# Column maximum of the router logits: read by VectorE from PSUM in two halves, behind ScalarE's half copies

## The reference, cut to what matters

```
x      = _layernorm(x, norm_g, norm_b)
se     = _layernorm(slot_embeds, slot_g, slot_b) * scale
logits = einsum('bnd,esd->bnes', x, se)          # 2 x 1024 tokens, 1024 slots
dispatch = softmax(logits, axis=1)               # over the 1024 tokens of a batch
combine  = softmax(logits over all 1024 slots)   # over a token's slots
slots = einsum('bnd,bnes->besd', x, dispatch)
... gate/up/down of 16 experts ..., out = combine @ eout
```

## Time and profile before

| | us |
|---|---|
| median of 3 runs | 600.85 (600.81 to 602.04) |
| profiled execution, its own time | 601.5 |
| its span, first to last instruction | 599.8 |
| PE, DVE, ACT, POOL busy in the span | 551.3, 483.7, 394.5, 320.3 |
| logits stage, from the first to the last copy L764 | 308.5 to 362.8 |
| dispatch stage, from the first to the last L1377 | 368.5 to 427.0 |

### The profile page before, as it was taken

One profiled execution on the slowest core, in us unless ns is written; L12 is line 12 of the kernel. 1 busy time (PEld: TensorE's weight loads), 2 busy tenths in 40 slices (PEclk: granted clock), 3 DMA queues, 4 the chain that ended last, 5 costly groups with the idle time before them and its releaser, 6 DMA issues.

```text
span 599.8 us, 11864 instructions
## 1 busy us (share of the span) xinstructions
PE 551.3 (92%) x3880; PEld 507.0 (85%) x3880; DVE 483.7 (81%) x1338; ACT 394.5 (66%) x1054; POOL 320.3 (53%) x327
## 2 busy tenths in 40 slices
PE   5889999999999999999889996999779999969998
PEld 3778999999999999999777765888658788869998
DVE  5888878787889889896859998999798999964553
ACT  3877959696968869695724435566476667555552
POOL 6463753544445644544559867565088999810000
PEclk9999999999999999999999997999889999989999
DMA  7602000000200000000013331050087888604552
GB/s 198 211 2 71 2 2 2 1 2 1 87 3 2 2 1 2 1 2 2 2 72 140 148 133 71 8 208 1 1 267 264 274 281 276 218 35 141 177 176 70
DMA packets 35372, 53.36 MB, mean 89 GB/s; under 512 B 6157, under 2 KB 21457, under 8 KB 35313
## 3 DMA queue, kind: packets, MB, share of 16 engines
q1 hardware_dynamic: 35313, 52.61, 26.3%
HBM read 42.12 MB, written 10.49 MB: 88 GB/s over the span
## 4 chain that ended last, share of the span: by engine, by line
PE 55%; DVE 21%; POOL 9%; ACT 7%; issue 7%; DMA 1%; SPq 0%; POOLq 0%; DVEq 0%; ACTq 0%
PE ps L1447 8%; PE ps L1316 8%; DVE w_gu_low L866 7%; PE ps L1267 6%; PE ps L1300 5%; PE ps L1377 5%; PE ps L1248 5%; PE ps L1279 3%; PE ps L1348 3%; PE ps L1302 2%; PE ps L1436 2%; POOL prob L595 2%; DVE wkq_low L1093 2%; DVE eo_high L1129 2%; ACT expo L726 2%
## 5 line engine op out<-in xcount | busy, mean ns | idle before, releaser
L595 POOL TENSOR_TENSOR prob<-expo,prec 128x512 f32<-128x512 f32 x64 | 66.7, 1043 | 97.3 <-DVE prec L982 96.1
L726 ACT ACTIVATE expo<-expo,nmin 128x154 f32<-128x154 f32 x256 | 106.2, 423 | 4.0 <-DVE nmin L971 3.6
L971 DVE CUSTOM_DVE_ANT_0 expo<-ps,maskb 128x154 f32<-128x154 f32 x256 | 69.1, 312 | 11.8 <-PE ps L1267 11.3
L656 POOL TENSOR_TENSOR wkq_low<-w_raw,wkq_high 128x1024 fp32r<-128x1024 f32 x16 | 51.3, 3207 | 24.5 <-ACT wkq_high L684 24.5
L1267 PE MATMUL ps<-kbd,qT_high 128*128 128x308 f32 x256 | 61.0, 322 | 0.2 <-ACT qT_high L665 0.2
L991 DVE TENSOR_TENSOR pT_low<-ps,pT_high 128x512 fp32r<-128x512 f32 (+1 forms) x96 | 57.3, 597 | 4.2 <-ACT pT_high L740 3.8
L740 ACT CAST pT_high<-ps 128x512 fp32r<-128x512 f32 (+1 forms) x96 | 49.1, 515 | 15.5 <-PE ps L1279 11.8
L665 ACT ACTIVATE oT_high<-ps,bv_c 128x256 fp32r<-128x256 f32 x64 | 29.9, 468 | 36.9 <-PE ps L1302 36.9
L726 ACT ACTIVATION_READ_ACCUMULATOR expo<-expo,nmin 128x1 f32 x256 | 50.3, 196 | 0.0
L866 DVE TENSOR_TENSOR w_gu_low<-w_raw,w_gu_high 128x1024 fp32r<-128x1024 f32 x18 | 46.9, 2615 | 1.2 <-ACT w_gu_high L684 1.2
L1267 PEld LDWEIGHTS ps<-kbd,qT_high 128*128 128x128 f32 x256 | 39.9, 190 | 0.8 <-issue 0.4
(11 more groups left out here) (217 smaller groups left out, 1823.2 us busy)
## 6 DMA issues: line engine op xcount, KB each, us to landing
logits_dram<-lsb SPq DMA_DIRECT2D x16, 512.0 KB, 2.6
w_raw<-in_L_ffn_Wg_dram SPq DMA_DIRECT2D x16, 512.0 KB, 4.4
w_raw<-in_L_ffn_Wu_dram SPq DMA_DIRECT2D x16, 512.0 KB, 4.6
w_raw<-in_L_ffn_Wd_dram SPq DMA_DIRECT2D x16, 512.0 KB, 4.3
lraw<-logits_dram SPq DMA_DIRECT2D x16, 512.0 KB, 3.7
out_dram<-outb SPq DMA_DIRECT2D x16, 128.0 KB, 1.7
x<-in_x_dram SPq DMA_DIRECT2D x1, 1792.0 KB, 13.6
wk_raw<-in_L_xattn_Wk_dram SPq DMA_DIRECT2D x2, 512.0 KB, 5.0
```

The costliest lines, as they stand in the source:

```text
L595: pool.tensor_tensor(prob[:, n % 2, :, heads, :], expo[:, n % 2, pp, :, :, 0:P], prec[:, n % 2, pp].unsqueeze(3).to_broadcast([P, 2, 2, P] ...
L656: pool.tensor_tensor(low, w_raw[:, i % RAW].rearrange("p (k n) -> p k n", k=KD if w == 0 else FT), high, ALU.subtract).then_inc(gate_low i ...
L726: ins = act.activation(row, row, ACT.Exp, scale=-1.0, bias=nmin[:, n % 2, pp, j, h:h + 1], accum_out=psums[:, n % 2, pp, j, h:h + 1])
L971: ins = dve.tensor_tensor_reduce(out=expo[:, n % 2, pp, j, h, :], in0=ps[:, s % NS, h * SK:(h + 1) * SK], in1=maskb[:, (2 * (n // QUADS) + ...
```

## The change

ACT copies each tile in two instructions of 512 columns, one for each bank, and raises `l_ready` after each. DVE waits for each half by itself and folds it into `colmax`, but reads the logits from the PSUM bank and no longer from `lsb`; for the first tile of a batch it copies the bank. `colmax_ready` is raised after the second half. PE's wait for the banks of tile i - 2 now asks for `colmax_ready` instead of `l_ready`, and so does the first expert's. The store waits for both halves. The row maximum still reads `lsb`.

```diff
-            sp.wait_ge(l_ready, i + 1)
+            sp.wait_ge(l_ready, 2 * (i + 1))
...
                 act.wait_ge(l_full, i + 1)
-                act.copy(lsb[:, i].rearrange("p (c n) -> p c n", c=2), ps[:, 2 * (i % 2):2 * (i % 2) + 2, :])\
-                    .then_inc(l_ready, 1)
+                for c in range(2):
+                    act.copy(lsb[:, i, c * 512:(c + 1) * 512], ps[:, 2 * (i % 2) + c, :]).then_inc(l_ready, 1)
...
-                dve.wait_ge(l_ready, i + 1)
-
                 b = i // TB
                 if i % TB:
                     dve.wait_ge(colmax_ready, i)
-                first = lsb[:, i] if i % TB == 0 else colmax[:, b]
-                dve.tensor_tensor(colmax[:, b], first, lsb[:, i], ALU.max).then_inc(colmax_ready, 1)
+                for c in range(2):
+                    dve.wait_ge(l_ready, 2 * i + c + 1)
+                    most, src = colmax[:, b, c * 512:(c + 1) * 512], ps[:, 2 * (i % 2) + c, :]
+                    if i % TB == 0:
+                        ins = dve.tensor_copy(most, src)
+                    else:
+                        ins = dve.tensor_tensor(most, src, most, ALU.max)
+                ins.then_inc(colmax_ready, 1)
...
-                    pe.wait_ge(l_ready, i - 1)
+                    pe.wait_ge(colmax_ready, i - 1)
...
-                    pe.wait_ge(l_ready, TILES)
+                    pe.wait_ge(colmax_ready, TILES)
```

## The result

The changed kernel took 595.01 us (median of 4 runs, 592.82 to 596.76), the kernel before 601.44 beside it (4 runs, 600.81 to 602.08). The ratio is 0.990, 95% interval 0.988 to 0.992: 6 us faster. The forecast was 596.2 with a range from 594.0 to 599.5, on a time before of 600.85. The profiled execution of the changed kernel took 595.16 with a span of 593.4, against 601.5 and 599.8.

A forecast was written before the change was run, and what follows sets the result against it. PE, DVE and POOL were taken as full at once in the logits stage, with DVE and POOL excluding each other over SBUF. Gains 0.7 + 0.3 + 1.4 + 2.2 = 4.6 us, from 600.85 to 596.2; range 594.0 to 599.5.

The forecast's parts named there:

- The root: DVE instructions with two SBUF operands and POOL instructions exclude each other; prediction wrong if POOL's lengths stay.
- Part 1: Engine costs per logits tile: two PSUM halves cost DVE 0.05 us more; its round is 3.08, the same as PE's.
- Part 2: Start of the logits stage: POOL's chain to PE's transposes no longer held up by the first maximum; gain 0.7 us.
- Part 3: Logits tiles 2 to 8: PE keeps its own 3.08 us a tile, six tiles 18.5 instead of 18.75; gain 0.3.
- Part 4: Logits tiles 9 to 14, where DVE is late: shorter diagonal and maxima; gain 1.4 us.
- Part 5: Into the dispatch stage: earlier x_low and three L641 in 7.2 us instead of 9.0; gain 2.2 us.
- Part 6: PE's new wait for the maximum of tile i - 2: at least 1.1 us spare, cost 0.
- The rival "DVE": Logits stage: non-overlapping halves make DVE's round 3.25 against PE's 3.08; 598.2 us; chance 0.20, shared with a stopped gain.
- The slower rival: Logits stage: a POOL instruction slips between two halves, 0.6 us a tile; 606.9 to 609.1, say 608; chance 0.05.
- The clock: First dispatch block: shorter PE idle time keeps its clock up, some 1.0 us comes back, 595.2; chance 0.10.

The follow-up runs named there:

- psum_whole: Kernel before, whole copies and whole 1024-column maxima kept, but the maxima read the PSUM banks: 594.53 us, ratio 0.990.
- sbuf_halves: Changed kernel, but the half maxima read lsb in SBUF and PE gets the banks back from ACT: 606.4 us, ratio 1.009 to the kernel before.
- dve_plus: Changed kernel plus one unused 256-column reduction on DVE per tile: 596.88 us, ratio 0.993 to the kernel before.
- no_shift: Kernel before with POOL's shift addition (L624) left out: 598.26 us, ratio 0.995.
- warm: Changed kernel plus 12 unused identity matmuls on PE ahead of its wait for the last maximum: 593.69 us, ratio 0.987 to the kernel before.
- exp_only: Kernel before with only the dispatch stage's exponentials put in PSUM: 593.22 us, ratio 0.987.
- exp_in_psum: Changed kernel plus dispatch exponentials written to the logits banks, both halves made from there: 586.91 us, ratio 0.977 to the kernel before.
- exp_psum_warm: Changed kernel plus dispatch exponentials in PSUM and 12 filling matmuls on PE: 587.99 us, ratio 0.977 to the kernel before.
- again: Changed kernel once more, unaltered: 595.18 us, ratio 0.990 to the kernel before.
- whole_and_exp: Whole copies, whole maxima from PSUM and dispatch exponentials in PSUM: 589.81 us, ratio 0.982 to the kernel before.

## Why the prediction was right, and where it was off

**The root was right.** DVE with two SBUF operands and POOL exclude each other; reading PSUM ends that. POOL's additions are 0.74, three L641 take 7.05 us (forecast 7.2), and `psum_whole` and `sbuf_halves` show that it is the operand and not the halves. The Trainium skill says in "SBUF — State Buffer", section "Who interferes with whom", that a DVE instruction with two SBUF inputs contends with a GpSimd instruction that reads SBUF. The runs agree: half a maximum has a mean of 1190 ns with two SBUF operands and of 685 with one in PSUM.

**Part 1, right in its price, and lucky in its balance.** The pair costs 1.29 us, as in the earlier trace rows, and DVE holds PE's pace, though with nothing to spare, as `dve_plus` shows. But DVE's round was reckoned at 3.08, the same as PE's, and PE's own is 3.00. DVE keeps up with that only because its round is shorter too: from `x2T_low` to the row maximum it takes 0.65 (320.98 to 321.63) and not 0.75, since the centring between them (L1046) takes 0.41 instead of 0.50. That POOL is the reason is likely, not shown: its instruction then under way ended 0.34 us after the centring's start before (322.34) and ends 0.14 after it now (321.45). Before, then after:

```profile
322.00 0.50 DVE L1046 TENSOR_SCALAR x2f<-x,mv,rstd 128x256 f32<-128x256 f32 x1
```

```profile
321.31 0.41 DVE L1046 TENSOR_SCALAR x2f<-x,mv,rstd 128x256 f32<-128x256 f32 x1
```

The prediction had neither of the two; that they are of one size is luck. The rule that speaks against it (the Trainium skill, "VectorE: DVE Perf Modes", section "The TRN2 errata": a dearer fixed cost from PSUM) is not seen here: 1221 ns with one operand in PSUM, 1.21 to 1.23 us with both in SBUF, for 1024 columns.

**Part 2, right:** 0.81 for 0.7. L611 is 0.20 us, as reckoned.

**Part 3 is the step that failed.** It says "PE keeps its own 3.08"; its own pace is 3.00, as after and as in `no_shift`. Rows 2 show transposes 3.08 apart with no wait in brackets. The wait stands in the rows of the weight loads (PEld), which I did not count: before, the transposes' weight load starts after 0.28 to 0.38 us of idle time, 0.1 us behind the end of POOL's addition, tile after tile; after, it follows without idle time. Before, then after:

```profile
323.77 1.66 POOL L624 TENSOR_TENSOR x2f<-x2f,shift 128x256 f32<-128x256 f32 x1
...
325.54 0.20 PEld L1332 LDWEIGHTS ps<-ident,x2f 128*128 128x128 f32 x2 [0.29 <-issue]
```

```profile
327.65 0.37 PEld L1336 LDWEIGHTS ps<-ident,x2f 128*128 128x128 f32 x2
```

The releaser in the brackets is no help: for some tiles it is "issue", for others `x2T_low`, never POOL. So I took a pace set by POOL for PE's. Six tiles at 3.00 give 0.72 instead of 0.3.

**Part 4: right in kind, two terms too small.** The first rows are of before, the second of after.

```profile
336.22 1.22 DVE L1065 TENSOR_TENSOR colmax<-lsb 128x1024 f32<-128x1024 f32 x1
...
349.80 1.65 POOL L623 TENSOR_TENSOR x2f<-x2f,gain 128x256 f32<-128x256 f32 x1 [3.19 <-DVE x2f L1046]
...
352.39 0.41 PE L1332 MATMUL ps<-ident,x2f 128*128 128x128 f32 x2 [0.17 <-POOL x2f L624]
```

```profile
334.76 1.28 DVE L1066 COPY colmax<-ps 128x512 f32<-128x512 f32 x2
336.67 0.69 DVE L1085 TENSOR_TENSOR diag<-ident,nb 128x512 f32<-128x512 f32 x1
...
345.16 0.42 DVE L851 TENSOR_TENSOR x2T_low<-ps,x2T_high 128x256 fp32r<-128x256 f32 x1
...
345.63 0.73 PE L1352 MATMUL ps<-wkq_high,x2T_high 128*128 128x512 f32 x2 [0.30 <-DVE x2T_low L851]
```

From the maximum of tile 8 to the `x2T_low` that tile 12 waits for, DVE's list took 11.63 us (336.22 to 347.85) and takes 10.40: 1.23, where the diagonal at 0.69 and the shorter maxima had been reckoned at 1.27. But tile 8's maximum also starts sooner after the transposes, 3.88 us (330.88 to 334.76) against 4.40: 0.52, taken as 0.1. DVE's maxima lagged further behind PE before: tile 7's started 1.20 us after its transposes (333.02 after 331.82) and starts 0.89 after them now (331.77 after 330.88). And from tile 12's matmuls to the copy of tile 13 it is 6.94 against 7.30 us: 0.36 that I had not seen. It is the exclusion once more: POOL's multiplication at 349.80 took 1.65 behind a maximum issued at 349.63, and PE waited for POOL's chain at 352.39, which it does not now. Together 2.11 for 1.4.

**Part 5, right:** 2.33 for 2.2. The low half still meets the third L641, and ends 1.1 us after it.

**Part 6, right:** the wait for `colmax` costs nothing that the profile shows.

**The sum** is 1.4 us short: 0.4 from the pace taken for PE's own, 0.4 from DVE's lateness ahead of tile 8, 0.36 from PE's wait for POOL after tile 12, and 0.2 in parts 2 and 5. The pace and the wait for POOL come from the exclusion, which reached further than I had followed it; what made DVE later is not taken apart by any run. The median of the runs, 595.0, lies 1.2 under the forecast; the kernel before measured 601.44 beside it, not 600.85, so the gain is 6.4 where 4.6 was forecast, and 0.4 of that lies outside the stage. The rival "DVE" fell, but by a few hundredths of a microsecond a tile. The slower rival fell for PSUM operands, and stands for SBUF ones: `sbuf_halves` took 606.4, and the rival's lower bound is by its own terms 606.7 (600.85 + 6.3 - 0.43), not 606.9. The clock fell as before, and cost about 0.25.

## What to carry to other kernels

Where DVE and POOL are both busy, look for pairs of rows of which one is long exactly until the other ends; if DVE's instruction can read one of its two operands from PSUM, where it often lies anyway, both run at their own length. Do not count on splitting the instruction as a cure: here two halves in SBUF were worse than one whole (606.4 against 601.2). And before an interval between two matmuls is taken for PE's own pace, look at its weight loads too, and at what ended just before them on the other engines: a wait of a tenth can stand there without its true releaser, and recur each round.

## What the runs showed of the hardware

**Reading PSUM cost DVE nothing that shows.** 1024 columns of fp32 took 1221 ns with one operand in PSUM and 1.21 to 1.23 us with both in SBUF; 512 columns took 685.

**The late stages come in two or three lengths, which go with PE's clock.** From the first matmul of the experts to the first of the output it is 106.0 us in the kernel before, `warm`, `exp_only`, `exp_in_psum`, `exp_psum_warm`, `dve_plus` and `no_shift`, and 107.6 in the changed kernel, `again`, `psum_whole`, `sbuf_halves` and `whole_and_exp`. From there to the end it is 64.0 in the kernel before, 62.5 in `warm`, `dve_plus` and `no_shift`, and 61.1 in the others. The windows of PE go with it: the granted clock is 0.50 from about 21 to 24 us into the expert stage in the five kernels with 107.6 and in none of the others, and it is 0.50 for the first 6 us of the output stage where that takes 64.0, for 3 us where it takes 62.5, and full speed from its start where it takes 61.1. In the changed kernel, whose first expert matmul is at 424.65 and first output matmul at 532.29:

```profile
444.60:446.60 2.00, 1.19 (x5) 0.70 1.00 361
446.60:448.60 2.00, 2.00 (x11) 0.50 0.89 281
...
532.29:534.29 2.00, 2.00 (x17) 1.00 0.00 0
```

and in the kernel before (429.78 and 535.84), in the same places:

```profile
450.40:452.40 2.00, 1.89 (x15) 1.00 0.89 306
...
535.84:537.84 2.00, 2.00 (x9) 0.50 0.00 0
```

In the changed kernel PE is idle for 0.8 of 2 us while the DMA engines are full, and the clock goes to 0.50 there; in the kernel before it stays at full speed there and is at 0.50 for the first 6 us of the output stage. So the profiled execution of before carries 2.9 us of output stage, and that of the changed kernel 1.6 us of expert stage, that are the clock's. Where the maximum reads its operand does not decide it alone: `exp_only` has the maxima of before and 61.1, `warm` and `dve_plus` have those of the change and 106.0. That is why the stages had to be compared one by one: the single executions of the changed kernel alone are up to 4 us apart. What decides which stage loses its clock was not tried, and stays open: there is one profiled execution of each kernel, and two of the changed one, which agree.
